# A Transformer block with a ternary MLP: the last group's first MLP is moved into the group before it, and all queues get a new order

## The reference

```python
x = x + attn_block(layernorm(x))      # first block
x = x + ternary_mlp(layernorm(x))     # second block

# first block, on u = layernorm(x)
q, k = elu(n @ Wq + bq) + 1, elu(n @ Wk + bk) + 1      # n = layernorm(u), 64 features
v = n @ Wv + bv
a = causal sum over k, v, divided by the causal sum of q.k
u = u + (a @ Wo + bo)
u = u + gelu(layernorm(u) @ W1 + b1) @ W2 + b2         # 256 -> 1024 -> 256

# second block, on z = layernorm(x)
h = gelu(z @ ternary(W_fc))                            # 256 -> 1024
y = layernorm(h) @ ternary(W_proj)                     # 1024 -> 256
```

## Time and profile before

| quantity | value |
|---|---|
| median of 3 runs | 449.51 us (448.89 to 450.82) |
| profiled execution | 450.32 us |
| its span, first to last instruction | 448.5 us |
| mean granted TensorE clock | 0.986 of full speed |
| PE busy | 425.4 us, 95% of the span |
| PEld busy | 388.0 us, 87% |
| DVE busy | 361.1 us, 81% |
| ACT busy | 324.6 us, 72% |
| POOL busy | 300.5 us, 67% |

### The profile page before, as it was taken

How to read it: one execution, slowest core, us unless ns; L and a number is a source line. 1 busy time by engine, 2 the same in 40 slices (tenths; PEclk the granted TensorE clock), 3 DMA queues, 4 the chain that set the end, 5 groups by cost and what they waited for, 6 DMA issues and landing times. The chain is left out here.

```text
span 448.5 us, 9187 instructions
## 1 busy us (share of the span) xinstructions
PE 425.4 (95%) x2910; PEld 388.0 (87%) x2910; DVE 361.1 (81%) x1156; ACT 324.6 (72%) x578; POOL 300.5 (67%) x268
## 2 busy tenths in 40 slices
PE   4999999999999999999999999999999999999892
PEld 3888888988989898988999899898989998989782
DVE  6797996886897888968897889978797858946686
ACT  4889558987498758986588847988388857963490
POOL 3684068596778559876689946895878521677384
PEclk9999998999999999999999999999999999999897
DMA  7324030100410021020301120120300000010011
GB/s 241 124 95 142 0 96 1 31 20 0 142 47 3 1 94 50 0 96 11 87 0 48 50 71 2 41 79 1 95 1 2 1 1 0 1 48 3 1 47 50
DMA packets 13521, 20.44 MB, mean 46 GB/s; under 512 B 2720, under 2 KB 11040, under 8 KB 12960
## 3 DMA queue, kind: packets, MB, share of 16 engines
q1 hardware_dynamic: 13472, 19.84, 13.7%
HBM read 15.62 MB, written 4.22 MB: 44 GB/s over the span
## 5 line engine op out<-in xcount | busy, mean ns | idle before, releaser
L1475 POOL TENSOR_TENSOR h<-h 128x512 f32<-128x512 f32 x56 | 72.5, 1295 | 8.8 <-ACT h L851 4.2
L292 PE MATMUL bank_y<-wf_hi,h_hi 128*128 128x256 f32 x224 | 63.4, 283 | 0.8 <-DVE h_lo L1091 0.6
L551 PE MATMUL bank_y<-wpj_t,g_hi 128*128 128x256 f32 x256 | 63.3, 284 | 0.1
L294 PE MATMUL bank_y<-wf_hi,h_lo 128*128 128x256 f32 x224 | 62.6, 279 | 0.0
L293 PE MATMUL bank_y<-wf_lo,h_hi 128*128 128x256 f32 x224 | 62.6, 279 | 0.0
L551 PE MATMUL bank_y<-wpj_t,g_lo 128*128 128x256 f32 x256 | 62.2, 280 | 0.0
L1453 POOL TENSOR_TENSOR rs<-ve,neg_half 128x2 f32<-128x2 f32 x32 | 22.5, 703 | 49.7 <-DVE ve L1028 45.8
L1091 DVE TENSOR_TENSOR h_lo<-bank_f,h_hi 128x512 fp32r<-128x512 f32 x45 | 30.5, 686 | 26.1 <-ACT h_hi L806 25.9
L551 PEld LDWEIGHTS bank_y<-wpj_t,g_hi 128*128 128x128 f32 x256 | 48.1, 188 | 2.2 <-issue 0.5
L551 PEld LDWEIGHTS bank_y<-wpj_t,g_lo 128*128 128x128 f32 x256 | 48.2, 188 | 1.2
L797 ACT ACTIVATE bank_f<-bank_f,f_bias 128x512 f32<-128x512 f32 x48 | 31.6, 662 | 20.0 <-PE bank_f L294 19.6
(11 more groups left out here) (330 smaller groups left out, 1471.3 us busy)
## 6 DMA issues: line engine op xcount, KB each, us to landing
out<-y_yc SPq DMA_DIRECT2D x15, 256.0 KB, 2.3
lines_b<-lines SPq DMA_DIRECT2D x6, 512.0 KB, 3.9
u<-in_xt SPq DMA_DIRECT2D x6, 512.0 KB, 3.6
x_even<-in_x SPq DMA_DIRECT2D x8, 256.0 KB, 2.9
x_odd<-in_x SPq DMA_DIRECT2D x8, 256.0 KB, 3.0
h<-in_f SPq DMA_DIRECT2D x1, 1024.0 KB, 7.7
y_yc<-in_f SPq DMA_DIRECT2D x1, 1024.0 KB, 10.0
h<-in_fc SPq DMA_DIRECT2D x1, 1024.0 KB, 6.1
```

Of the source, the lines that this page charges most:

```text
L292: pe.matmul(ps, w[0], r[0], start=start, stop=False, skip_group_check=skip)
L294: return pe.matmul(ps, w[1], r[0], start=False, stop=stop, skip_group_check=skip)
L551: mm = pe.matmul(out_half(t), gr[part][:, (8 * g + m) % RG, t * P:(t + 1) * P], wpj[:, m, :], start=(m == 0 and part == 0 and t % 2 == 0), ...
L1475: pool.tensor_tensor(squares[:, 0, :], squares[:, 0, :], square_tile(m), ALU.add).then_inc(s["squares_sum"], 1)
```

## The change

**Places in the ring.** The three bank functions take the group, and a common count of places replaces them. Group 7's f1 gets the places between fc(6, 3) and fc(6, 4):

```diff
+        def f1_slot(g, m):
+            return 18 * g + m - (0 if g < G - 1 else KH - EARLY)
+        def z3_slot(g, h):
+            return 18 * g + 8 + h
+        def fc_slot(g, m):
+            return 18 * g + 10 + m + (KH if g == G - 2 and m >= EARLY else 0)
+        def f1_bank(g, m):
+            return ring[f1_slot(g, m) % 3]
...
+            def slot_free(n):
+                for g in range(G):
+                    for m in range(KH):
+                        if f1_slot(g, m) == n - 3:
+                            pe.wait_ge(s["h_lo"], 8 * g + m + 1)
+                        if fc_slot(g, m) == n - 3:
+                            pe.wait_ge(s["g_lo"], 8 * g + m + 1)
+                            pe.wait_ge(s["h_added"], 8 * g + m + 1)
```

```diff
-            def f1b():
+            def f1b(part):
...
-                for m in range(KH):
+                for m in (range(FIRST), range(FIRST, KH))[part]:
...
-            def fill():
```

**Variance.** The square is scaled by 1/32 on ACT, so that its sum is already divided by 1024:

```diff
+            def ln4_mean(g):
...
+                for t in range(T):
+                    dve.tensor_scalar(h_mean[:, t:t + 1], h_total[:, t:t + 1], -1.0 / H, None, ALU.mult).then_inc(s["h_mean"], 1)
+                dve.wait_ge(s["h_mean"], 4 * g + 4)
+                for t in range(T):
+                    dve.scalar_tensor_tensor(h_less[:, t:t + 1], h_mean[:, t:t + 1], h_mean[:, t:t + 1], eps[:],
+                                             ALU.mult, ALU.subtract).then_inc(s["h_less"], 1)
...
             def ln4_var(g):
-                    dve.tensor_scalar(h_mean2[:, t:t + 1], h_total[:, t:t + 1], h_total[:, t:t + 1], -1.0 / (H * H),
-                    dve.tensor_scalar(ve[3][:, t:t + 1], h2_total[:, t:t + 1], 1.0 / H, h_mean2[:, t:t + 1],
-                    dve.tensor_scalar(ve[3][:, t:t + 1], ve[3][:, t:t + 1], 0.0, LN_EPS, ALU.max, ALU.add).then_inc(s["ln4_ve"], 1)
+                    dve.tensor_scalar(ve[3][:, t:t + 1], h2_total[:, t:t + 1], h_less[:, t:t + 1], LN_EPS,
+                                      ALU.subtract, ALU.max).then_inc(s["ln4_ve"], 1)
```

**Order.** All five lists are new. The places that the prediction speaks of (PE first, then ACT, DVE, POOL):

```diff
 PE, front
-  qkb(); tu(0, 0); tu(0, 1); wvo_mm(); qk_mm(0); bvo(); fill(); tu(1, 0); v_mm(0, 0); v_mm(0, 1); tu(1, 1); scores(0)
-  qk_mm(1); attend(0, 0); attend(0, 1); attend(0, 2); attend(0, 3); f1b(); scores(1); theta_sum(0); tz2(0, 0)
-  tz2(0, 1); v_mm(1, 0); f1h(0, 0, 0); f1h(0, 0, 1); f1h(0, 1, 0); f1h(0, 1, 1); f1(0, 2); v_mm(1, 1)
+  qkb(); tu(0, 0); tu(0, 1); wvo_mm(); qk_mm(0); bvo(); f1b(0); v_mm(0, 0); tu(1, 0); v_mm(0, 1); tu(1, 1); scores(0)
+  f1b(1); qk_mm(1); attend(0, 0); attend(0, 1); attend(0, 2); attend(0, 3); theta_sum(0); tz2(0, 0); scores(1)
+  theta_sum(1); tz2(0, 1); v_mm(1, 0); f1h(0, 0, 0); f1h(0, 0, 1); f1h(0, 1, 1); f1h(0, 1, 0); f1(0, 2); f1(0, 3)
 PE, group 0's seam
-  attend(1, 0); attend(1, 1); cpj(); attend(1, 2); spread(); tz3(0, 0); tz3(0, 1); fch(0, 0, 0); fch(0, 0, 1)
-  fch(0, 1, 0); fch(0, 1, 1); fc(0, 2); attend(1, 3); proj(0, 0)
+  attend(1, 0); attend(1, 1); attend(1, 2); cpj(); tz3(0, 0); attend(1, 3); tz3(0, 1); spread(); fch(0, 0, 0)
+  fch(0, 0, 1); fch(0, 1, 1); fch(0, 1, 0); fc(0, 2); proj(0, 0)
 PE, group 2's seam: attend(3, 0) now ahead of tz3(2, 0), formerly behind it
 PE, the end (new)
+  fch(6, 1, 1); fch(6, 1, 0); fc(6, 2); attend(7, 3); fc(6, 3); proj(6, 0); proj(6, 1); tz2(7, 0); proj(6, 2)
+  tz2(7, 1); proj(6, 3); f1h(7, 0, 0); f1h(7, 0, 1); f1h(7, 1, 1); f1h(7, 1, 0); f1(7, 2); f1(7, 3); f1(7, 4)
+  f1(7, 5); f2(7, 0, 1); f2(7, 1, 1); f1(7, 6); f1(7, 7); f2(7, 0, 0); f2(7, 1, 0); fc(6, 4); fc(6, 5); f2(7, 2, 0)
...
+  f2(7, 7, 0); fc(6, 6); f2(7, 2, 1); f2(7, 3, 1); f2(7, 4, 1); f2(7, 5, 1); f2(7, 6, 1); f2(7, 7, 1); fc(6, 7)
+  proj(6, 4); proj(6, 5); tz3(7, 0); ths(6); tz3(7, 1); proj(6, 6); tsq(6); fch(7, 0, 0); fch(7, 0, 1); proj(6, 7)
+  fch(7, 1, 0); fch(7, 1, 1); fc(7, 2); fc(7, 3); proj(7, 0)
...
+  proj(7, 5); proj(7, 6); ths(7); tsq(7); proj(7, 7)
 ACT, front
-  tables(); u_norm(0, 0); u_norm(0, 1); wqk_hi(); u_hi(0, 0); u_hi(0, 1); wvo_copy(); wf1_hi(0); wf1_hi(1); wf1_hi(2)
-  wf1_hi(3); u_norm(1, 0); wvo_hi(); qk_exp(0); u_norm(1, 1); qk_hi(0); k_dup(0); u_hi(1, 0); v_hi(0, 0); v_hi(0, 1)
-  ...; k_dup(1); abs_part(0); abs_part(1); ae_hi(1); z2_norm(0, 0); z2_norm(0, 1); wf2_hi(3); z2_hi(0, 0)
+  tables(); gelu_table(); ln3_hi(); wqk_hi(); u_norm(0, 0); u_norm(0, 1); u_hi(0, 0); u_hi(0, 1); wvo_copy()
+  wf1_hi(0); wf1_hi(1); wf1_hi(2); qk_exp(0); wvo_hi(); u_norm(1, 0); u_norm(1, 1); qk_hi(0); v_hi(0, 0); u_hi(1, 0)
+  k_dup(0); wf1_hi(3); ...; abs_part(0); qk_hi(1); abs_part(1); k_dup(1); z2_norm(0, 0); abs_part(2); abs_part(3)
+  ae_hi(1); z2_norm(0, 1); z2_hi(0, 0); z2_hi(0, 1)
 ACT, the end (new)
+  gelu3(6, 7); square(6, 7); g_hi(6, 7); z3_norm(7, 0); z3_norm(7, 1); z3_hi(7, 0); z3_hi(7, 1); gelu3(7, 0)
 DVE: selectors(), ln3_lo() and qk_bias_add() from later to the start; qk_max(0) ahead of wvo_add()
 DVE, the end
-  h_sum(7); h2_sum(7); ln4_var(7); centre(7, 0); centre(7, 1); centre(7, 2); last_output(0); last_output(1)
-  centre(7, 3); last_output(2); last_output(3)
+  h_add(6, 7); ln3_shift(7, 1); g_lo(6, 7); z3_odd(7, 1); h_sum(6); z3_lo(7, 0); ln4_mean(6); z3_lo(7, 1); h2_sum(6)
+  ln4_var(6); centre(6, 0)
...
+  h_sum(7); ln4_mean(7); h2_sum(7); centre(7, 0); ln4_var(7); centre(7, 1); centre(7, 2); centre(7, 3)
+  last_output(0); last_output(1); last_output(2); last_output(3)
 POOL, the end
-  output(6, 0); sq_add(7, 1); output(6, 1); sq_add(7, 2); ...; sq_add(7, 7); y_cpj(7); ln4_rstd(7)
+  output(6, 0); sq_add(7, 1); sq_add(7, 2); output(6, 1); sq_add(7, 3); ...; sq_add(7, 7); y_cpj(7); ln4_rstd(7)
```

More of the change, by code:

```diff
@@ L850, in square @@
                     act.wait_ge(s["tern"], 4)
[L851 removed]
+                act.activation(square_tile(m), fc_bank(g, m)[:], ACT.Square, scale=1.0 / 32).then_inc(s["squared"], 1)
             def order():
[L854 to L855 removed]
@@ L916, in order @@
-                square(7, 5); gelu3(7, 6); g_hi(7, 6); square(7, 6); gelu3(7, 7); square(7, 7); g_hi(7, 7)
+                tables(); gelu_table(); ln3_hi(); wqk_hi(); u_norm(0, 0); u_norm(0, 1); u_hi(0, 0); u_hi(0, 1)
+                wvo_copy(); wf1_hi(0); wf1_hi(1); wf1_hi(2); qk_exp(0); wvo_hi(); u_norm(1, 0); u_norm(1, 1); qk_hi(0)
+                v_hi(0, 0); u_hi(1, 0); k_dup(0); wf1_hi(3); u_hi(1, 1); v_hi(0, 1); ae_hi(0); ad_hi(0); af_hi(0)
+                n1(0); wf2_hi(0); wf2_hi(1); wf2_hi(2); qk_exp(1); wf2_hi(3); abs_part(0); qk_hi(1); abs_part(1)
@@ new lines, in order @@
+                k_dup(1); z2_norm(0, 0); abs_part(2); abs_part(3); ae_hi(1); z2_norm(0, 1); z2_hi(0, 0); z2_hi(0, 1)
+                ad_hi(1); gelu(0, 0); v_hi(1, 0); h_hi(0, 0); gelu(0, 1); h_hi(0, 1); gelu(0, 2); h_hi(0, 2)
+                gelu(0, 3); h_hi(0, 3); gelu(0, 4); af_hi(1); h_hi(0, 4); v_hi(1, 1); n1(1); gelu(0, 5); gelu(0, 6)
+                h_hi(0, 5); h_hi(0, 6); gelu(0, 7); h_hi(0, 7); u_hi(2, 0); z3_norm(0, 0); z3_norm(0, 1); z3_hi(0, 0)
+                rows(); z3_hi(0, 1); spread_copy(); gelu3(0, 0); square(0, 0); g_hi(0, 0); gelu3(0, 1); gelu3(0, 2)
@@ new lines, in order @@
+                z2_hi(2, 1); gelu3(1, 7); square(1, 7); g_hi(1, 7); u_hi(3, 0); gelu(2, 0); gelu(2, 1); h_hi(2, 0)
+                h_hi(2, 1); u_hi(3, 1); gelu(2, 2); h_hi(2, 2); gelu(2, 3); h_hi(2, 3); gelu(2, 4); n1(3); qk_exp(3)
+                qk_hi(3); k_dup(3); h_hi(2, 4); gelu(2, 5); h_hi(2, 5); ae_hi(3); gelu(2, 6); h_hi(2, 6); gelu(2, 7)
+                h_hi(2, 7); af_hi(3); ad_hi(3); v_hi(3, 0); z3_norm(2, 0); v_hi(3, 1); z3_norm(2, 1); z3_hi(2, 0)
+                z3_hi(2, 1); u_hi(4, 0); gelu3(2, 0); square(2, 0); gelu3(2, 1); g_hi(2, 0); g_hi(2, 1); square(2, 1)
@@ new lines, in order @@
+                square(3, 7); z2_hi(4, 1); g_hi(3, 7); gelu(4, 0); h_hi(4, 0); u_hi(5, 0); u_hi(5, 1); gelu(4, 1)
+                gelu(4, 2); h_hi(4, 1); h_hi(4, 2); gelu(4, 3); h_hi(4, 3); qk_exp(5); qk_hi(5); k_dup(5); gelu(4, 4)
+                h_hi(4, 4); n1(5); gelu(4, 5); gelu(4, 6); h_hi(4, 5); h_hi(4, 6); gelu(4, 7); h_hi(4, 7); ae_hi(5)
+                ad_hi(5); af_hi(5); v_hi(5, 0); z3_norm(4, 0); v_hi(5, 1); z3_norm(4, 1); z3_hi(4, 0); z3_hi(4, 1)
+                gelu3(4, 0); square(4, 0); g_hi(4, 0); gelu3(4, 1); g_hi(4, 1); square(4, 1); gelu3(4, 2)
@@ new lines, in order @@
+                gelu3(5, 7); square(5, 6); square(5, 7); g_hi(5, 7); gelu(6, 0); gelu(6, 1); h_hi(6, 0); gelu(6, 2)
+                h_hi(6, 1); h_hi(6, 2); gelu(6, 3); h_hi(6, 3); gelu(6, 4); qk_exp(7); gelu(6, 5); gelu(6, 6)
+                qk_hi(7); k_dup(7); h_hi(6, 4); h_hi(6, 5); h_hi(6, 6); af_hi(7); ae_hi(7); gelu(6, 7); h_hi(6, 7)
+                n1(7); ad_hi(7); v_hi(7, 0); z3_norm(6, 0); v_hi(7, 1); z3_norm(6, 1); z3_hi(6, 0); z3_hi(6, 1)
+                gelu3(6, 0); g_hi(6, 0); square(6, 0); gelu3(6, 1); gelu3(6, 2); square(6, 1); g_hi(6, 1)
@@ L1568, in order @@
+                sq_add(7, 1); sq_add(7, 2); output(6, 1); sq_add(7, 3); sq_add(7, 4); sq_add(7, 5); sq_add(7, 6)
```

614 lines of the change are left out of this document (292 added, 322 removed).

## The result

The changed kernel takes 465.11 us (median of 4, 464.23 to 465.87), the kernel before beside it 449.2: 1.0347 of it, 95% interval 1.0315 to 1.0379. It is 16 us slower, where I had forecast 445.8 and a range of 441.3 to 450.5. The profiled execution took 465.2, span 463.5.

The account below looks back on a forecast made before the run. TensorE was taken to bound the middle, with DVE, ACT and POOL bounding the ends. Front 2.9, first MLP -1.6, seam -2.7, middle -0.7, end -1.6 sum to -3.7: 446.6 us profiled, 445.8 median, range 441.3 to 450.5.

Parts of the forecast that it names:

- Middle: Groups 1 to 6: attend(3,0) ahead of tz3(2,0) saves its wait, other reordering and shorter variance worth nothing; -0.7 us.
- The rival that went to the slower side: Middle seams open with waits and half clock; two such seams give +1.8 us, three +4.6, 454.1 us; chance 0.13.
- Rest of the first MLP: Group 0's first MLP: selectors() moves to the start, so DVE no longer delays h_lo; -1.6 us.
- Front: Start to v_mm(1,0): ACT's new order and a chain through tz2(0,0) and scores(1) delay v_mm(1,0); +2.9 us.
- the upper bound of +4.7: Front: the cost if PE's empty 4.8 us before tz2 are followed by a half-clock stretch.
- Seam: After group 0's first MLP: attend(1,3) between tz3(0,0) and tz3(0,1) removes the wait (1.05) and half clock (1.7); -2.7 us.
- End: Last group: interleaving changes gelu3(7,0)'s start, POOL's squares and the tail; three terms, together -1.6 us.
- The first term: End: gelu3(7,0) can start 52.3 us after v_mm(7,0) instead of 54.0, with waits of 0.75, 0.95 and 0.75; -1.7 us.
- The second: End: POOL's squares queue behind output(6,0), ending 16.6 us after gelu3(7,0) starts instead of 15.17; +1.4 us.
- The third: Tail from the squares' end to DVE's last operation: 5.3 us instead of 6.65, y_cpj(7) deciding; -1.3 us.
- That POOL and ACT would set the last stage either way: Rival for the end: interleaving does nothing, the end is worth nothing, 447.4 us; chance 0.10.
- a point between 0.76 and 1.05: Middle seams, slower rival: a PE wait of 0.76 us brought no half clock, 1.05 did, so the deciding point lies between.

Follow-up runs that it names:

- the first experiment: Changed kernel with the four h_less operations as tensor_scalar (mean as pointer, epsilon immediate) instead of scalar_tensor_tensor: 451.8 us, 1.005 of the kernel before.
- the variance alone: Kernel before, order untouched, with only the shorter variance: 470.72 us (1.047) with h_less as scalar_tensor_tensor, 450.34 us (1.0017) as tensor_scalar.
- n1(1) back: Changed kernel with h_less as tensor_scalar and n1(1) on ACT put back behind h_hi(0,7): 450.3 us, 1.0034 of the kernel before.
- end alone: Kernel before with the shorter variance, h_less as tensor_scalar, and the changed order, ring places, banks and waits only from v_mm(7,0) on: 448.29 us (0.998).
- last experiment: Kernel before with tensor_scalar variance and the changed end, plus the changed PE order at group 0's seam, attend(1,3) between the tz3s: 449.68 us (1.0012).
- undoing the end: Changed kernel with h_less as tensor_scalar and n1(1) put back, and before's order, places and waits from v_mm(7,0) on: 452.96 us (1.009).
- ternary operations ahead: Changed kernel with the second to fourth ternary operations on DVE taken ahead of group 2's LayerNorm statistics: 468.9 us (1.0432).
- two inputs, another operation: Changed kernel with h_less as tensor_tensor, mean times mean, both inputs in SBUF, epsilon left out: 460.47 us (one execution).

## Why the prediction was wrong

**Middle: the step that failed.** "The four operations fewer per group in the variance are DVE work beside a full PE: nothing." I counted the operations and didn't look at their operands. Before, all sixteen had one tensor input; now four of twelve have two, in SBUF. Before's trace has no DVE operation with two tensor inputs in SBUF beside a POOL operation of 512 columns, so the cost couldn't be read off; "nothing" had no row behind it. POOL's operations took 1.25 to 1.42 us each, so a wait for one in front of each of the four would have been an upper bound of about 5 us per group. The runs showed up to 3.91 us for four, 11.4 us in the middle, and 13.3 in the median that go with the other form: shown by the first experiment, and by the variance alone from the other side. Nor did the -0.7 come: with the other form the middle is 297.0 against 296.9.

The Trainium skill, "SBUF — State Buffer", section "SBUF: two separate sides", says that GpSimd and a VectorE operation with two SBUF inputs take a shared pair of ports as an exclusive lock, for the whole instruction. The traces agree: the h_less wait for whole POOL operations, 1.32 us at most for one column, and 0.57 for all four with one input. That the engines meet only through semaphores, as I wrote at the start, doesn't hold for DVE and POOL: no semaphore stands between h_less and the POOL operations that it waited for.

The rival that went to the slower side had the right stretch and the wrong mechanism: waits at the seams' tz3 were not what opened. PE stood in f1 and f2, waiting for h_lo (once for centre) behind h_less; the half clock followed two of these waits, at 154.89 and 261.96.

**Rest of the first MLP: -1.6, measured +3.6.** selectors() did leave. "ternary and threshold keep their cost and only move" failed: beside xs(0) and n1o(1) the two operations of a pair took up to 1.60 and 2.20, against 0.75 and 1.28. And I named nobody behind n1(1), which now stood ahead of gelu(0,5) and waited 3.24 us for POOL. With n1(1) back the stretch is 0.1 shorter than before, so of the -1.6 little was there.

**Front: +2.9, measured +2.6.** Right, by its path, and in part by luck: k_dup(0) ended at 22.51 (22.6 forecast), scores(0) began at 22.61, tz2(0,0) at 34.81 (35.7), v_mm(1,0) at 39.14 (39.5), with a clock of 0.67 from 30 to 40. So the half clock that the upper bound of +4.7 asked for did come; tz2(0,0) was 0.9 sooner than forecast, and from there to v_mm(1,0) it took 4.3 us instead of 3.8. One wait was not in it: PE stood 2.96 us at theta_sum(0), for abs_part(1), and so reached tz2(0,0) little before z2 was there. Before's front in all five lists takes the 2.3 back (end alone); which of them it needs is open, as is what the split of the bias products does by itself.

The load of the tables ran from 15.12 to 16.40, and qk_exp(0) began at 16.42, 1.0 earlier than before: it fills the gap that I had given it, and no drain follows.

**Seam: -2.7, measured -1.75.** The wait and the half clock are gone, as forecast; 0.9 comes back as a wait of proj(0,0) for g_lo. The last experiment shows that attend(1,3) in the gap isn't enough by itself; that ACT's order, with rows() later, is what it lacks, is read from the lists and was not run.

**End: -1.6, measured -1.2 from v_mm(7,0) on.** The first term gained more: gelu3(7,0) starts 51.4 us after v_mm(7,0) (385.75 to 437.16), not 52.3, since the three waits are 0.46, 0.46 and 0.19. The second was right: POOL's squares end 16.15 after it (16.6). The third was wrong in sign, for the same reason as the middle: h_less at 453.97 takes 2.09 beside y_cpj(7), ln4_rstd(7) waits 1.83 for DVE where I had it follow y_cpj(7) directly, and the tail from the squares' end grows from 6.65 to 7.08. With the other h_less DVE ends 4.3 after the last product, against 5.8 here and 5.4 before. That POOL and ACT would set the last stage either way is excluded by undoing the end, +2.7.

## What to carry to other kernels

Price an operation by its operands, not by its size alone: beside a busy POOL, a DVE operation of one column with two tensor inputs in SBUF can cost as much as POOL's operation (1.32 us), while four with a pointer and an immediate do the same work in 0.57. What a new order costs is not in the steps that it moves but in those queued behind them: for each wait that moves, name the chain of engines back to its source. When a large change loses, undo its parts one at a time; here the part that loses and the part that gains sit in different stretches, and the median shows only their sum.

## What the runs showed of the hardware

The form with one tensor input is safe here on one column, not on 1024: as tensor_scalar four h_less took 0.57 beside POOL, but the ternary tensor_scalar took 1.60 instead of 0.74. What sets the two apart was not tested. Nor does every POOL operation hold DVE: in the changed kernel's block at 204.47 the first h_less took 0.76, until POOL's operation of 512 columns had ended, and the other three 0.21 to 0.23, beside POOL's power on two columns.

POOL is held as well: its pair n1o(1), 2.48 us where DVE had no such operation (ternary operations ahead), took 4.10 between the ternary ones, and xs(0) 3.10 instead of 2.52. DVE and POOL take turns: in 3.78 us four h_less got in between three POOL operations that ran without a visible gap.

The length of PE's wait alone doesn't set the half clock. A wait of 1.05 was followed by it, one of 2.24 too (clock 0.83 from 150 to 160), but one of 1.51 at 315.34 was followed by 1.00 from 315 to 345, one of 1.45 at group 0's seam (last experiment) by 1.00 too, and one of 2.16, at the place of the 2.24, by 1.00 (two inputs, another operation). So a point between 0.76 and 1.05 from which a wait decides, as the prediction has it, is not what the runs show; what does decide stays open.
